# Quantised feed-forward of layer 2: its weights' and rows' FP4 rounding spread over three stages, and a new order of work in its own

## The chip, the cores and the metric

One core of a Trainium2 chip runs the whole model in one launch. The metric is the time of one execution on the device, in microseconds; before and after are compared by the median of several executions.

## The reference, cut to what matters

Four layers, each a cross attention and a feed-forward, on 2048 tokens of 256 numbers (x is 2 x 1024 x 256). Layer 0's feed-forward is a soft mixture of 8 dense experts (top 2 of the weights), layer 1's a top-2 mixture of gated experts with the rows dispatched, layer 3's a shared part and routed experts. Layer 2's is the quantised one:

```python
def fp4_quant_dequant(x):                       # blocks of 16 along the last axis
    xb = x.reshape(shape[:-1] + (shape[-1] // 16, 16))
    scale = jnp.maximum(jnp.max(jnp.abs(xb), axis=-1, keepdims=True) / 6.0, 1e-12)
    idx = jnp.searchsorted(_MID, jnp.abs(xb / scale))
    return (_GRID[idx] * jnp.sign(xb / scale) * scale).reshape(shape)

def fp4_linear(x, w):
    return jnp.einsum('bsk,nk->bsn', fp4_quant_dequant(x), fp4_quant_dequant(w))

gate = fp4_linear(x, w_gate)                    # w_gate, w_up: 704 x 256
y = fp4_linear(x, w_up)
h = jax.nn.silu(gate) * y
return fp4_linear(h, w_down)                    # w_down: 256 x 704
```

Its input x is the layer norm of the running sum. Three things are rounded to FP4: the weights, the normed rows, and the hidden rows h.

## The kernel before, in words

Tokens lie in 16 tiles of 128 (NT), four tiles to a group (NG = 4 groups). The running sum X (16 tiles x 256) and a second array Y of that size stay in SBUF, beside two arenas: FA (float32, 9216 numbers for each partition) and RA (28672). Every product in float32 is made of three matmuls of a high and a low part (split_matmuls, line 300 on; L307 is the matmul): ScalarE writes the high part, VectorE subtracts it from the value to get the low part. So each operand of TensorE passes through both engines.

The program is a list of phases, and each phase has one function for each engine; each engine's order is written out by hand, and semaphores join them. At the end of a phase all engines count on a barrier; SyncE (SP, which issues most transfers) and GpSimd wait there for all others, the compute engines go on where a phase says only_loads_wait. Each queue works in its written order, so an instruction that waits holds up all behind it on its engine.

The stages that matter here, in the order in which they run:

- Soft experts of layer 0 (gelu_block, line 1758; the jobs are lines 2045 to 2061 on VectorE and job(q, t) on TensorE). A job is one tile of tokens and two experts: six matmuls of 512 columns into one of five PSUM banks (RING = 5), then two scalar_tensor_tensors on VectorE (L2050) that add it, weighed, to X. There are four rounds (q) of 16 jobs; between the first and the second come eight bias jobs. In the last round VectorE also takes the next norm's moments (L199).
- Gated experts of layer 1 (experts, line 1410): 23 blocks (16 of 256 rows, 7 of 128). In a block TensorE makes 48 matmuls up, the transposes of the next block's rows (L1646) and 24 matmuls down for the block before. VectorE splits 1 MB of up weights (L1624) and 0.5 MB of down weights (L1693), and makes the hidden products. WeightsOfFp4 (line 501) works between its blocks: six pieces of 704 numbers, three parts each, one part after each of the blocks 1 to 18 (vector, line 542): part 0 is L548 to L553 (largest of each block of 16, scales, reciprocal, division), part 1 L555 to L557 (the exponent by a bit mask, times a magic number, added to force the rounding), part 2 L559 and L560 (subtract the magic, times the scale). GpSimd's queue loads and stores the pieces (lines 527 to 540) between the gathers and scatters of rows. The rounded pieces go to a DRAM tensor, which SP loads back (prefetch, L565) when layer 2's attention starts.
- Attention of layer 2 (attention(2), line 585): a loop of one tile a slot. VectorE's part of a slot (work, from line 870) is L876, L877 for one tile, L889, L891 for the one before, L907, L908 for the one ahead, L911, and the next norm's moments (L199, L206, L208) and minus_mean (L217). ScalarE writes the normed tiles (L225) of the norm that follows, eleven of the 16 within the loop, the last five in finish_scalar in the next stage. GpSimd has only rstd (L271), a power, once a group.
- The quantised stage (fp4_feed_forward, line 2468). First: TensorE turns the gate and up weights (L2676), ScalarE copies the high parts (L2561), VectorE makes the low parts (L2616); the down weights the same (L2682, L2563, L2564, L2618, L2620); the four groups of normed rows are quantised by VectorE (quantise_xn, line 2603, through Quantiser: L2523, L2524, L2527, L2528, L2529, L2532, then a multiplication by the magic number on ScalarE, L2556, then L2536 to L2538), turned by TensorE (L283) and split (L290, L297). Then eight pairs of tiles: gate_up for each tile (24 matmuls of 352 columns), silu on ScalarE (L2576), product on VectorE (L2629), quantising of the pair's hidden rows on VectorE (the same Quantiser on 1408 numbers), turning them (L2707), low and high parts, and the product down (L2717). The keys and the query weights of layer 3's attention (ahead[3], class Ahead) are prepared ahead of the pairs.

## Time and profile before

| | us |
|---|---|
| median of the runs | 1635.72 (1634.01 to 1636.18) |
| the profiled execution's own time | 1638.06 |
| its span, first to last instruction | 1636.3 |
| PE busy | 1386.8 (85%) |
| DVE busy | 1240.5 (76%) |
| ACT busy | 772.5 (47%) |
| POOL busy | 337.0 (21%) |

PE is TensorE, DVE VectorE, ACT ScalarE, POOL GpSimd, SP SyncE. Times in a row are microseconds from the start of the span. Line numbers are those of the kernel before. A busy share is a mean over stages with different limits. The granted clock (PEclk) of TensorE is 1.00 at 2.4 GHz and 0.50 at 1.2 GHz; values between are a stretch with both.

### The profile page before, as it was taken

How to read it: one execution, taken by the hardware profiler on the slowest of the kernel's cores; microseconds unless marked ns; L12 is line 12 of the kernel's file. 1: busy time of each engine (PE TensorE's matmuls, PEld its weight loads, DVE VectorE, ACT ScalarE, POOL GpSimd, SP SyncE). 2: the span in 40 equal slices, each digit the busy share in tenths (PEclk: the TensorE clock that was granted, in tenths of full speed). 3: DMA queues.
4: the chain of work that ended last, by engine and by line, in shares of the span. 5: the costliest groups of instructions: out<-in, count | busy, mean ns of one | idle time of the engine just before them, and what ended most of it. 6: DMA issues, size and time to landing. Idle time of an engine off the chain costs nothing.

```text
span 1636.3 us, 25886 instructions
## 1 busy us (share of the span) xinstructions
PE 1386.8 (85%) x9890; PEld 1266.5 (77%) x9890; DVE 1240.5 (76%) x2386; ACT 772.5 (47%) x1318; POOL 337.0 (21%) x278
## 2 busy tenths in 40 slices
PE   4897997798995599999399459968998999999995
PEld 4786895586883599999379358966886888999995
DVE  5696778777896589997379779976886857888773
ACT  4445442113455266666355442325445225676673
POOL 2241001000000157764100000000000013454342
PEclk9898998799998599998699879988998999999997
DMA  4232100000002478886300000000002016777784
GB/s 139 91 104 89 45 1 1 1 0 10 1 1 110 150 211 233 244 224 174 124 1 1 7 0 1 1 10 1 1 1 104 1 65 233 233 214 220 219 241 116
DMA packets 44926, 148.23 MB, mean 91 GB/s; under 512 B 11651, under 2 KB 22582, under 8 KB 35062
## 3 DMA queue, kind: packets, MB, share of 16 engines
q1 hardware_dynamic: 28886, 122.04, 21.9%
q0 software_dynamic: 15936, 24.78, 7.8%
q8 instruction: 67, 1.10, 0.3%
q14 instruction: 37, 0.30, 0.1%
HBM read 126.03 MB, written 22.87 MB: 91 GB/s over the span
## 4 chain that ended last, share of the span: by engine, by line
PE 56%; DVE 26%; ACT 8%; issue 5%; DMA 2%; POOLq 1%; SPq 1%; POOL 0%; ACTq 0%; DVEq 0%
PE PS L307 37%; PE PS L1005 6%; PE PS L966 3%; PE PS L989 3%; DVE RA L1624 2%; PE PS L1240 1%; DVE RA L1693 1%; ACT Y L225 1%; ACT RA L1617 1%; DVE FA L1661 1%; PE PS L998 1%; DVE RA L297 1%; PE PS L982 1%; DVE RA L1673 1%; POOLq L2764 1%
## 5 line engine op out<-in xcount | busy, mean ns | idle before, releaser
L307 PE MATMUL PS<-RA 128*128 128x256 f32 (+3 forms) x6204 | 942.7, 311 | 74.9 <-DVE RA L397 16.2
L307 PEld LDWEIGHTS PS<-RA 128*128 128x128 f32 x6204 | 859.5, 197 | 130.3 <-issue 34.5
L1551 POOL DMA_INDIRECT sum_rows<-Y,KT x78 | 158.6, 2033 | 193.1 <-ACT Y L1592 162.2
L271 POOL TENSOR_TENSOR rstd<-vareps,neghalf 128x4 f32<-128x4 f32 x36 | 36.8, 1023 | 707.2 <-DVE vareps L208 330.0
L1005 PE MATMUL PS<-VBF,FA 128*128 128x136 f32 x1024 | 136.1, 287 | 4.4 <-ACT FA L771 4.2
L1540 POOL DMA_INDIRECT Y<-normed_rows,KT x78 | 89.8, 1151 | 219.7 <-DVE KT L1333 158.5
L1005 PEld LDWEIGHTS PS<-VBF,FA 128*128 128x128 f32 x1024 | 124.8, 192 | 10.3 <-ACT FA L771 6.8
L771 ACT ACTIVATE FA<-PS 128x1024 f32<-128x1024 f32 x64 | 65.7, 1027 | 103.9 <-PE PS L966 103.9
L1570 ACT ACTIVATE FA<-PS,unit_bias 128x256 f32<-128x256 f32 (+1 forms) x184 | 71.7, 445 | 78.2 <-PE PS L307 65.4
L1624 DVE TENSOR_TENSOR RA<-FA,RA 128x2048 fp32r<-128x2048 f32 x46 | 105.2, 2288 | 4.4 <-ACT RA L1584 3.7
L1693 DVE TENSOR_TENSOR RA<-FA,RA 128x1024 fp32r<-128x1024 f32 (+1 forms) x46 | 80.9, 1759 | 24.8 <-ACT RA L1617 24.8
L283 PE MATMUL PS<-ident,Y 128*128 128x128 f32 x256 | 43.4, 328 | 60.2 <-ACT Y L225 33.0
L1584 ACT ACTIVATE RA<-FA 128x2048 fp32r<-128x2048 f32 x46 | 88.1, 1914 | 12.8 <-DMA FA<-in_eup 12.8
L283 PEld LDWEIGHTS PS<-ident,Y 128*128 128x128 f32 x256 | 36.8, 172 | 68.8 <-issue 45.9
L779 ACT ACTIVATE FA<-FA 128x1024 f32<-128x1024 f32 x64 | 67.5, 1055 | 39.9 <-DVE FA L908 34.6
L225 ACT ACTIVATE Y<-X,minus_mean,rstd 128x256 f32<-128x256 f32 x96 | 51.9, 590 | 63.1 <-DVE minus_mean L217 62.7
L966 PE MATMUL PS<-ident,FA 128*128 128x128 f32 x512 | 68.3, 277 | 12.0 <-ACT FA L779 12.0
L2050 DVE SCALAR_TENSOR_TENSOR X<-PS,coef,X 128x256 f32<-128x256 f32 x128 | 61.3, 482 | 19.7 <-PE PS L307 17.3
L966 PEld LDWEIGHTS PS<-ident,FA 128*128 128x128 f32 x512 | 58.5, 143 | 12.8 <-ACT FA L779 12.8
L1617 ACT ACTIVATE RA<-FA 128x1024 fp32r<-128x1024 f32 (+1 forms) x46 | 68.4, 1488 | 0.0
L989 PE MATMUL PS<-RA 64*128 64x256 f32 x768 | 63.0, 299 | 1.1 <-DVEq L902 1.1
L989 PEld LDWEIGHTS PS<-RA 64*128 64x128 f32 x768 | 50.3, 189 | 15.5 <-issue 13.8
(295 smaller groups left out, 1874.9 us busy)
## 6 DMA issues: line engine op xcount, KB each, us to landing
FA<-in_eup SPq DMA_DIRECT2D x46, 1024.0 KB, 7.0
FA<-in_edown SPq DMA_DIRECT2D x23, 1024.0 KB, 6.3
FA<-in_edown SPq DMA_DIRECT2D x23, 512.0 KB, 4.1
FA<-in_fside SPq DMA_DIRECT2D x16, 512.0 KB, 3.6
sum_rows<-X SPq DMA_DIRECT2D x2, 2048.0 KB, 7.4
normed_rows<-Y SPq DMA_DIRECT2D x2, 2048.0 KB, 10.2
fp_rows<-FA POOLq DMA_DIRECT2D x6, 352.0 KB, 6.8
FA<-fp_rows SPq DMA_DIRECT2D x1, 2112.0 KB, 11.9
```

The costliest lines, as they stand in the source:

```text
L283: ins = pe.transpose(self.bank(g, k)[:, j * P:(j + 1) * P], self.normed(g, j)[:, 0, k * P:(k + 1) * P], ident[:, :])
L307: ins = pe.matmul(dst, stat(a, k), mov(b, k), start=(first and n == 0), stop=(last and n == len(todo) - 1))
L966: ins = pe.transpose(PS[:, 4 + c // 4, (c % 4) * P:(c % 4 + 1) * P], probs[t % BUFS][:, c * P:(c + 1) * P], ident[:, :])
L989: ins = pe.matmul(PS[:, 2 * p + r, k * COLS:(k + 1) * COLS], qs[rows, a, k, t * P:(t + 1) * P], kb[rows, b, m, k, r * COLS:(r + 1) * COLS] ...
L1005: ins = pe.matmul(PS[:, 6, k * VC:(k + 1) * VC], pt[:, 4 * (c // 2) + 2 * k + c % 2, :], VB[:, t // HT, 4 * k + c, :], start=(c == 0), sto ...
L1540: pool.indirect_dma_start(out=rows_in[p][:, t, :], out_offset=None, in_=normed_rows, in_offset=bass.IndirectOffsetOnAxis(ap=source_of[:, c ...
L1551: pool.indirect_dma_start(out=sum_rows, in_=rows_out[p][:, t, :], in_offset=None, compute_op=ALU.add, out_offset=bass.IndirectOffsetOnAxis ...
L1570: ins = act.activation(h32[s % RING][:, c * BR:c * BR + w], bank[:, c * BR:c * BR + w], ACT.Relu, bias=unit_bias[:, p, 2 * s + c:2 * s + c ...
L1584: act.activation(up[q][:, 0], raw_up[q], ACT.Copy).then_inc(up_hi, 1)
L1617: act.activation(down[p][:, 0], raw_down[p], ACT.Copy).then_inc(down_hi, 1)
L1624: dve.tensor_tensor(up[q][:, 1], raw_up[q], up[q][:, 0].bitcast(F32), ALU.subtract).then_inc(up_ready, 1)
L1693: dve.tensor_tensor(down[p][:, 1], raw_down[p], down[p][:, 0].bitcast(F32), ALU.subtract).then_inc(down_ready, 1)
```

## The change

1. Weights. Pieces 0 to 3 are rounded in the soft experts, pieces 4 and 5 stay in the gated experts (blocks 1 to 6 of VectorE). SP loads and stores the early pieces; VectorE has twelve slots, one every third job from job 13 (job 13 in the first round, the others at jobs 16, 19, ..., 46, counted 16 to a round); GpSimd does the two multiplications with a value for each block, and VectorE the rest. There are two buffers for four pieces, and the slot at job 31 waits for the loads of pieces 2 and 3. The slots' order is: scales of piece 0, scales of piece 1, units of 0, rounding of 0, units of 1, rounding of 1, then the same for 2 and 3.
2. Rows. A class RowsOfFp4 splits a group's quantising: VectorE makes the scales and, in one step of two operations after the bit mask, the magic number; GpSimd does the division, the addition, the subtraction and the last multiplication. Groups 0 and 1 are done within the attention's loop (VectorE at slots 11, 12, 15 and 16; GpSimd between its rstds), groups 2 and 3 in the stage. ScalarE's magic step for rows is gone.
3. The stage's order. Only group 0 is turned before the first gate_up; the down weights are turned behind the first gate_up, in other PSUM banks; group 1 behind the second; groups 2 and 3 within the first pair; layer 3's query weights and keys in pairs 0 and 1. Buffers move in FA and Y.
4. Some semaphores are shared between stages instead of being new ones; their counts change (w_hi, w_ready, the shares).

```diff
             PIECES, PARTS, FIRST_BLOCK = 6, 3, 1
+            EARLY, FIRST_JOB, JOBS_APART = 4, 13, 3
+            def sync_early(self, sp, split):
+                sp.wait_ge(*split)
+                for n in range(2):
+                    sp.dma_start(self.early_x[n], self.source(n)).then_inc(self.early_in, 16)
+                for n in range(self.EARLY):
+                    sp.wait_ge(self.by_pool, self.multiplied(n))
+                    sp.dma_start(self.done_rows[:, n, :], self.early_x[n % 2]).then_inc(self.early_stored, 16)
+                    if n + 2 < self.EARLY:
+                        sp.wait_ge(self.early_stored, 16 * (n + 1))
+                        sp.dma_start(self.early_x[n % 2], self.source(n + 2)).then_inc(self.early_in, 16)
+            def gpsimd_early(self, pool):
+                for n in range(self.EARLY):
+                    x = self.early_x[n % 2]
+                    pool.wait_ge(self.by_vector, self.scaled(n))
+                    if n:
+                        pool.wait_ge(self.by_pool, self.multiplied(n - 1))
+                    pool.tensor_tensor(self.blocks(self.early_u), self.blocks(x), self.of_block(self.early_rs[n % 2]), ALU.mult
+                                       ).then_inc(self.by_pool, 1)
+                    pool.wait_ge(self.by_vector, self.rounded(n))
+                    pool.tensor_tensor(self.blocks(x), self.blocks(self.early_u), self.of_block(self.early_sc[n % 2]), ALU.mult
+                                       ).then_inc(self.by_pool, 1)
+            def vector_early(self, dve, steps, job):
+                slot, off = divmod(job - self.FIRST_JOB, self.JOBS_APART)
+                order = [(first + i, part) for first in range(0, self.EARLY, 2)
+                         for i, part in ((0, 0), (1, 0), (0, 1), (0, 2), (1, 1), (1, 2))]
...
+                n, part = order[slot]
+                if part == 0:
+                    dve.wait_ge(self.early_in, 32 * (n // 2 + 1))
+                    if n >= 2:
+                        dve.wait_ge(self.by_pool, self.multiplied(n - 2))
+                    self.scales(dve, steps, self.early_x[n % 2], self.early_am, self.early_sc[n % 2], self.early_rs[n % 2]
+                                ).then_inc(self.by_vector, 1)
+                elif part == 1:
+                    dve.wait_ge(self.by_pool, self.divided(n))
+                    self.units_of(dve, steps, u, m)
+                else:
+                    steps(dve.scalar_tensor_tensor(u, m, self.MAGIC, u, ALU.max, ALU.add))
+                    dve.scalar_tensor_tensor(u, m, self.MAGIC, u, ALU.max, ALU.subtract).then_inc(self.by_vector, 1)
...
+        class RowsOfFp4:
+            EARLY = 2
...
+            def vector_scales(self, dve, steps, g):
+                dve.wait_ge(fp4_norm.xn_ready, fp4_norm.groups + g + 1)
+                steps(dve.tensor_reduce(self.am, self.blocks(self.x(g)), AX, ALU.max, apply_absolute_value=True))
+                dve.tensor_scalar(self.sc[g], self.am, -1.0 / 6.0, -1e-12, ALU.mult, ALU.min)
...
+                dve.reciprocal(self.rs[g], self.rs[g]).then_inc(self.scaled, 1)
+            def vector_magic(self, dve, steps, g):
+                dve.wait_ge(self.divided, g + 1)
+                steps(dve.tensor_scalar(self.m[g].bitcast(U32), self.u.bitcast(U32), 0x7F800000, None, ALU.bitwise_and))
+                dve.tensor_scalar(self.m[g], self.m[g], self.MAGIC, self.MAGIC, ALU.mult, ALU.max).then_inc(self.magic, 1)
+            def gpsimd(self, pool, g):
+                u, m, x = self.u, self.m[g], self.x(g)
+                steps = Steps(pool, self.done, 3 * g)
+                pool.wait_ge(self.scaled, g + 1)
+                pool.tensor_tensor(self.blocks(u), self.blocks(x), self.of_block(self.rs[g]), ALU.mult).then_inc(self.divided, 1)
+                pool.wait_ge(self.magic, g + 1)
+                steps(pool.tensor_tensor(u, m, u, ALU.add))
+                steps(pool.tensor_tensor(u, m, u, ALU.subtract))
+                steps(pool.tensor_tensor(self.blocks(x), self.blocks(u), self.of_block(self.sc[g]), ALU.mult))
...
 (attention, GpSimd, l == 2)
+                        for g in range(NG):
+                            following.pool_rstd(pool, g)
+                            if 1 <= g <= rows_of_fp4.EARLY:
+                                rows_of_fp4.gpsimd(pool, g - 1)
 (attention, VectorE, at the end of a slot)
+                    if l == 2 and t in (11, 15):
+                        rows_of_fp4.vector_scales(dve, steps, (t - 11) // GT)
+                    if l == 2 and t in (12, 16):
+                        rows_of_fp4.vector_magic(dve, steps, (t - 12) // GT)
 (soft experts)
+                        weights_of_fp4.vector_early(dve, steps, NT * q + t)
 (quantised stage, ScalarE)
                 finish_scalar(act, norm, 0)
+                rows_of_fp4.wait_done(act, rows_of_fp4.EARLY - 1)
                 finish_scalar(act, norm, 1)
...
+                    if p == 0:
+                        norm.scalar(act, 2)
+                        norm.scalar(act, 3)
+                        ahead[3].scalar_query_weights(act)
+                        ahead[3].scalar_keys_hi(act)
+                    if p == 1:
+                        ahead[3].scalar_keys(act)
 (quantised stage, VectorE)
+                rows_of_fp4.vector_scales(dve, steps, 2)
+                norm.vector_lo(dve, 0)
+                rows_of_fp4.vector_scales(dve, steps, 3)
+                rows_of_fp4.vector_magic(dve, steps, 2)
...
                 product(0, 0)
+                down_weights_lo()
                 product(0, 1)
+                norm.vector_lo(dve, 1)
+                rows_of_fp4.vector_magic(dve, steps, 3)
...
+                    if p == 0:
+                        norm.vector_lo(dve, 2)
+                        norm.vector_lo(dve, 3)
+                        ahead[3].vector_query_weights(dve)
+                        ahead[3].vector_keys_lo(dve)
 (quantised stage, TensorE)
                 turn_x(0)
+                pe.wait_ge(wt_lo, 2)
+                gate_up(0, 0)
+                turn_down_weights()
+                gate_up(0, 1)
+                pe.wait_ge(wt_lo, 3)
                 turn_x(1)
-                gate_up(0, 0)
-                turn_x(2)
-                gate_up(0, 1)
-                turn_x(3)
                 gate_up(1, 0)
...
+                    if p == 0:
+                        turn_x(2)
+                        turn_x(3)
+                        pe.wait_ge(norm.xt_ready, 1 + KC * (norm.groups + NG))
```

## Rows read from the trace of the kernel before

**Rows 1.** Windows: us, busy (instructions) of each engine, PEclk, DMA share, GB/s.

```profile
373.70:394.60 20.90, 18.86 (x88) 15.47 (x87) 20.10 (x67) 6.43 (x13) 3.02 (x3) 1.00 0.00 1
...
587.50:714.20 126.70, 121.06 (x990) 118.51 (x989) 117.36 (x186) 86.94 (x170) 88.86 (x57) 1.00 0.83 232
834.00:900.00 66.00, 66.00 (x589) 60.67 (x588) 59.73 (x117) 35.51 (x47) 2.01 (x2) 0.98 0.00 1
917.00:976.00 59.00, 25.17 (x116) 23.21 (x116) 43.32 (x54) 26.88 (x50) 0.00 (x0) 0.71 0.02 5
```

**Rows 2.** Timeline of VectorE, soft experts: start, us, engine, line, instruction [idle before].

```profile
298.79 5.56 DVE L2050 SCALAR_TENSOR_TENSOR X<-PS,coef,X 128x256 f32<-128x256 f32 x12
...
341.48 1.00 DVE L2050 SCALAR_TENSOR_TENSOR X<-PS,coef,X 128x256 f32<-128x256 f32 x2 [0.35 <-PE PS L307]
```

**Rows 3.** Timeline of VectorE, one weight piece in the gated experts.

```profile
701.96 0.88 DVE L548 TENSOR_REDUCE Y<-FA 128x44 f32<-128x704 f32 x1
...
703.66 0.89 DVE L553 TENSOR_TENSOR Y<-FA,Y 128x704 f32<-128x704 f32 x1
...
713.29 0.89 DVE L557 SCALAR_TENSOR_TENSOR Y<-Y 128x704 f32<-128x704 f32 x1
```

**Rows 4.** GpSimd's groups by line: busy us, mean ns of one, idle before.

```profile
L696 POOL TENSOR_TENSOR FA<-FA,small 128x1024 f32<-128x1024 f32 x16 | 30.5, 1904 | 67.3 <-DVE small L905 67.3
```

**Rows 5.** Transfers: issues, KB each, median us from issue to landing.

```profile
FA<-in_fside SPq DMA_DIRECT2D x16, 512.0 KB, 3.6
...
fp_rows<-FA POOLq DMA_DIRECT2D x6, 352.0 KB, 6.8
```

**Rows 6.** Timeline of VectorE, gated experts: L1624 of one block and 13 blocks later.

```profile
587.51 2.29 DVE L1624 TENSOR_TENSOR RA<-FA,RA 128x2048 fp32r<-128x2048 f32 x1
...
714.21 2.29 DVE L1624 TENSOR_TENSOR RA<-FA,RA 128x2048 fp32r<-128x2048 f32 x1
```

**Rows 7.** Chain of work that ended last, layer 3's experts: start, us, what.

```profile
1387.85 11.52 PE PS L307 x96
```

**Rows 8.** Timeline of TensorE, half blocks: the transposes between up and down.

```profile
742.86 0.41 PE L1646 MATMUL PS<-ident,Y 128*128 128x128 f32 x2
...
763.16 0.41 PE L1646 MATMUL PS<-ident,Y 128*128 128x128 f32 x2
...
770.52 0.41 PE L1646 MATMUL PS<-ident,Y 128*128 128x128 f32 x2
```

**Rows 9.** Timeline of VectorE: a late slot of the attention, then group 0's quantising.

```profile
909.60 0.26 DVE L876 RECIPROCAL small<-PS 128x16 f32<-128x16 f32 x1 [1.15 <-PE PS L1005]
...
916.98 1.21 DVE L2523 TENSOR_REDUCE FA<-Y 128x64 f32<-128x1024 f32 x1
...
919.14 1.23 DVE L2529 TENSOR_TENSOR FA<-Y,FA 128x1024 f32<-128x1024 f32 x1
920.40 0.69 DVE L2532 TENSOR_SCALAR FA<-FA 128x1024 uint32<-128x1024 uint32 x1
```

**Rows 10.** Timeline of all engines, start of the quantised stage.

```profile
917.10 2.07 ACT L225 ACTIVATE Y<-X,minus_mean,rstd 128x256 f32<-128x256 f32 x4 [3.19 <-DVE minus_mean L217]
...
922.09 2.56 ACT L2561 ACTIVATE RA<-PS 128x1408 fp32r<-128x1408 f32 x2
...
925.88 3.15 DVE L2616 TENSOR_TENSOR RA<-PS,RA 128x1408 fp32r<-128x1408 f32 x2
929.08 2.82 PE L2682 MATMUL PS<-ident,FA 128*128 128x128 f32 x12 [12.64 <-DVE RA L2616]
...
946.79 5.05 PE L307 MATMUL PS<-RA 128*128 128x352 f32 x24
...
976.29 4.07 PE L307 MATMUL PS<-RA 128*128 128x352 f32 x24 [1.86 <-DVE FA L2629]
```

**Rows 11.** Timeline of VectorE: where the first and the second pair's quantising start.

```profile
976.06 1.61 DVE L2523 TENSOR_REDUCE FA<-FA 128x88 f32<-128x1408 f32 x1
...
989.62 1.61 DVE L2523 TENSOR_REDUCE FA<-FA 128x88 f32<-128x1408 f32 x1
```

More of the change, by code:

```diff
@@ L520, in source, with blocks, of_block, scales @@
                 return A["fp4_down"][:, n - (self.PIECES - KC), :]
+            def blocks(self, v):
+                return v.rearrange("p (b i) -> p b i", i=FB)
+            def of_block(self, v):
+                return v.unsqueeze(2).to_broadcast([P, FI // FB, FB])
+            def scales(self, dve, steps, x, am, sc, rs):
+                steps(dve.tensor_reduce(am, self.blocks(x), AX, ALU.max, apply_absolute_value=True))
+                dve.tensor_scalar(sc, am, -1.0 / 6.0, -1e-12, ALU.mult, ALU.min)
+                more = 1.0 + 2.0 ** -22
+                steps(dve.tensor_scalar(rs, am, more / 6.0, more * 1e-12, ALU.mult, ALU.max))
+                return dve.reciprocal(rs, rs)
@@ L2239, in shared_feed_forward @@
             before = 2
+            halves_before = before + KC
             norm = relu_norm
@@ L2446, in tensor @@
                 go_down(0, 3)
-                pe.wait_ge(w_ready, before + 2)
+                pe.wait_ge(w_ready, halves_before + 2)
                 go_up(1, 0)
@@ L2484, in fp4_feed_forward @@
             h = fview(2048, 3, PT * FI)
-            act_g = fview(6336, 2, FI)
-            scale, rscale, amax = (fview(7808 + n * P, P) for n in range(3))
+            act_g = fview(7296, 2, FI)
+            scale, rscale, amax = (fview(n * P, P) for n in range(3))
             yf = Y[:, :, :].rearrange("p t d -> p (t d)")
-            units, magic = (yf[:, o:o + 2048] for o in (0, 2048))
+            units = yf[:, 0:PT * FI]
+            magic_of = lambda p: yf[:, 2048:2048 + PT * FI] if p else h[:, 2, :]
             MAGIC = 1.5 * 2.0 ** 22
-            x_units, x_magic = fview(0, GT * D), fview(GT * D, GT * D)
             q_done = sem(n_ + "done")
@@ L2548, in fp4_feed_forward, with gpsimd @@
             tile_of = lambda p, i: PT * p + i
+            def gpsimd(pool):
+                for g in range(rows_of_fp4.EARLY, NG):
+                    rows_of_fp4.gpsimd(pool, g)
             def scalar(act):
                 finish_scalar(act, norm, 0)
+                rows_of_fp4.wait_done(act, rows_of_fp4.EARLY - 1)
                 finish_scalar(act, norm, 1)
@@ L2653, in vector @@
                     dve.wait_ge(h_done, PT * (p + 1))
-                    q = Quantiser(steps, h[:, p % 3, :], units, magic)
+                    q = Quantiser(steps, h[:, p % 3, :], units, magic_of(p))
                     q.normalise()
@@ L2678, in tensor, with turn_down_weights @@
                     ins.then_inc(wt_ready, 1)
[L2679 to L2684 removed]
+                def turn_down_weights():
+                    pe.wait_ge(norm.xt_ready, 1 + KC * (norm.groups + 1))
+                    for c in range(CK):
+                        for k in range(KC):
+                            ins = pe.transpose(turned_d[0:CW[c], c * D + k * P:c * D + (k + 1) * P], raw_down[:, k, c * P:c * P + CW[c]], ident[:, :])
+                    ins.then_inc(wt_ready, 1)
                 def turn_x(g):
[L2687 removed]
+                    rows_of_fp4.wait_done(pe, g)
                     norm.tensor(pe, g)
```

169 lines of the change are left out of this document (87 added, 82 removed).

## The prediction

> **What bounds the kernel now.** First the windows by stage. In the gated experts' loop VectorE is busy 117.36 of 126.70 us, TensorE 121.06, at full clock: the DMA share is 0.83, so both engines are near their limit there [rows 1]. In the soft experts (lines 2045 to 2073) the bound changes: for the first three quarters VectorE waits for TensorE before every job (0.35 us), and in the last quarter, where the next norm's moments are taken too, it is busy 20.10 of 20.90 [rows 1, 2]. In layer 2's attention loop it is busy 59.73 of 66.00; in the 59 us ahead of the quantised stage's pairs it is busy 43.32 and TensorE only 25.17, at 0.71 of the full clock [rows 1]. That last stretch is a chain through four engines, not a busy engine. Then the timelines of those four places, for where VectorE waits and for whom. The profiled execution took 1638.06 us (span 1636.3), 2.3 over the median of 1635.72; I work out a difference and apply it to the median. A measurement of this kernel tells about 0.2% (3.3 us) from no change.
>
> **Part 1: four of six weight pieces move into the soft experts.** A piece costs VectorE there: the scales 1.70 us (start of L548 to start of L553 [rows 3]), the units about 1.1 (two tensor_scalars, at 704/1024 of the price in part 3 and a gap each), two scalar_tensor_tensors of 0.89 with 0.04 between, so 1.85 [rows 3]. Two multiplications go to GpSimd, at 704/1024 of 1.90, 1.31 us each [rows 4]. That is 4.6 us of VectorE for each piece, 18.4 for four, in twelve slots, one every third job. What is there to cover it: a TensorE-bound job takes 1.36 us, back to back VectorE needs 5.56/12 x 2 = 0.93, so 0.43 is free [rows 2]. The slot at job 13 has two jobs behind it before the bias rows, on which TensorE waits: 1.7 - 0.9 = 0.8 is exposed. The other eleven slots hold 16.7 us, the 32 jobs of the second and third quarter free 13.8: 2.9 are left, and nothing in the last quarter takes them back [rows 1].
> A new wait: the slot at job 31 needs pieces 2 and 3, and piece 3 is loaded only after piece 1 is stored, which GpSimd finishes after the slot at job 28. On SP's queue: 1.31 multiply, a 352 KB store, a wait for it, a 352 KB load. The nearest idle-queue transfer took 3.6 us for 512 KB; under the experts' traffic 352 KB took 6.8 [rows 5]. The queue is idle here, so I take 3.6 and 3.4, 8.5 us with semaphores, from one store alone to 6.8 twice (15). Three jobs at 0.93 pass meanwhile: VectorE waits 8.5 - 2.8 = 5.7 us. Behind this wait stand all later jobs; TensorE's five buffers don't help, because VectorE itself has no time left to catch up. Sum 0.8 + 2.9 + 5.7 = **+9 us** (ends +5 and +16). SP has nothing else queued until the stage ends, and GpSimd's next item, the next norm's rstd, comes after the last slot.
> A sentence on a page: by the Trainium skill, page "DMA: Bandwidth & Descriptors", section "Anatomy of one DMA", a transfer costs about 2.0 us plus its bytes over 436 GB/s, 2.8 for 352 KB, which would make this part 7.5; that fit is for GpSimd's queue.
>
> **Part 2: the gated experts keep two pieces, in blocks 1 to 6.** Whole blocks now take (714.21 - 587.51)/13 = 9.75 us [rows 6]. TensorE alone needs 72 matmuls of 0.12 and four transposes, some 0.5: 9.1 [rows 7, 8]. Blocks 7 to 15 become TensorE's: at most 0.65 each; at least what TensorE is idle now, 5.64/13 = 0.43 [rows 1]. I take 0.6, nine times, 5.4. In the half blocks the transposes of three blocks lie 20.30 us apart for two periods and 7.36 for the third; that third is a half block with no piece at full clock, and the 20.30 hold a piece and a fall of the clock [rows 8]. With no piece and the clock held, a half block takes 7.4: 5.5 us off the two in the 20.30, and some 2 off the two before them. If the fall stays, 4 in all. I take 6. Sum **-11.5** (-8 to -14). GpSimd issues four stores and four loads less; its queue ends nothing here, so that is 0.
>
> **Part 3: two groups of rows within the attention loop.** VectorE's scales take 919.14 - 916.98 = 2.16, the magic step two tensor_scalars of 0.69, 1.4 [rows 9]. At slots 11 and 12 the loop has no gap, so 2.0 + 1.4. At slot 15 there is 1.15 us of idle ahead of L876 [rows 9]: 1.0 is left. At slot 16 the gap is shorter; 0.7. Sum **+5** (+3 to +8).
>
> **Part 4: the quantised stage.** Two groups' quantising leaves VectorE altogether, the two others' but for scales and magic step (3.6 each). But the stretch is a chain, so I follow it, from VectorE's end of the attention (0). GpSimd's last three operations on group 1 at 1.9 start 2 us before: they end at 4.3. Its rstd of group 3 is queued behind them: 5.5 (it was 1.1). ScalarE's four tiles wait for both: 7.7. The two weight copies, 2.56: 10.4. VectorE's low halves, the second 1.6 later: 12.3 [rows 4, 10]. Scales of group 2, 2.2: 14.5. The low half of group 0: 15.8. gate_up 5.0, as the first one took after such a start: 20.8 [rows 10]. Weights of down turned, 2.8: 23.6 [rows 10]. gate_up 5.4 (my estimate, between 4.1 at full clock and 8.1 at half, near the row of 5.05): 29.0. Silu and product, 1.7, and gate_up 5.4: 36.2; silu and product: the first pair starts at 38. Before, it started at 976.06, with the attention's end 1.2 us ahead of 916.98, so after 60.3 [rows 9, 11]: -22.3.
> Back in: pair 0. Groups 2 and 3 are turned behind gate_up(2, 0), whose result needs 44 + 4.1 = 48; silu, ScalarE's copy, four low halves and the layer 3 weights on VectorE end at 54, then it rounds (5): the next pair starts at 60, 22 us after the first, which was 13.6 [rows 11]: +8.3. ScalarE's work on layer 3's keys now sits between pairs 1 and 2 and delays a silu; VectorE waited for nothing there: I take +1.3. The six later pairs don't change. Stage: **-12.7** (-16 to -4).
>
> **Sum**: 9 - 11.5 + 5 - 12.7 = -10.2 us.
>
> **Rivals.** (a) GpSimd and VectorE in each other's way: layer 0 runs GpSimd's 1.90 us operation beside VectorE, every one alike, but not beside a VectorE operation with two operands in SBUF [rows 4]. If such operations exclude each other, each that meets GpSimd waits up to 1.9 us: L891 in two slots, the magic steps, the first pair's normalise, some 2 to 6, say +4: -6, 1629.5. For it: the change puts twelve GpSimd operations of 1024 beside VectorE. Against it: most stand where VectorE waits anyway.
> By the Trainium skill, page "SBUF — State Buffer", section "SBUF: two separate sides", the two engines share a pair of ports as an exclusive lock, which VectorE takes with two SBUF inputs or in its 2-port mode: that is this rival, and no row here shows it either way.
> (b) Experts don't give it back: ScalarE or the queues end the blocks (DMA share 0.83 of the stretch already [rows 1]), 9 x 0.2 and the clock's fall stays: -5 in place of -11.5. With part 1 at 11 us: -2, 1634.
> (c) Slower: TensorE stays at its lower clock. It is idle 13 us ahead of the first gate_up (12.64 before a stretch at 0.71 now [rows 1, 10]). A gate_up at the lower clock is 8.1 against my 5.0 to 5.4 for three, and 4.1 for the four of the first two pairs: 9 + 16 = 25 on the chain, less 1 or 2 that VectorE's own work covers. The net is then +13, 1649. It decides from about 13 us, that is if most of these seven are slow. Against it: the first gate_up after such a start took 5.05, the one of the first pair 4.07 [rows 10].
> (d) That it doesn't do what it says: the diff does move the work, the slots are compiled in and each has its semaphore, so I give this nothing of its own; a time within 0.2% would come by (b), where the parts cancel.
>
> **Chances.** Forecast 0.48, (a) 0.22, (b) 0.17, (c) 0.13. The forecast is the median less 10: 1625.7 us. Its own range is 1616 to 1632; (a) and (b) reach 1636; cutting off (c) and 5 parts in 100 at the low end gives 1614 to 1638. Faster by over 0.2% (below 1632.4): most of the forecast and of (a), 0.3 of (b): 0.70. Within 0.2%: 0.17. Slower: (c), 0.13.
>
> **What would show it.** Right: VectorE's L2050 jobs stand back to back from job 16, one wait of 4 to 7 us on a DMA at job 31, the stage ends 9 us later; whole blocks from the seventh at 9.1 to 9.2 and no fall of the clock in the half blocks; the attention 5 us longer; GpSimd busy some 4 us into the stage, the first pair 38 us after the attention and the second 22 after that. Wrong: blocks still at 9.7; GpSimd operations over 1.9 or VectorE's two-operand ones stretched, which is (a); gate_ups at 8 us, which is (c).

## The result, and the profile after

The kernel before took 1635.92 us (median of 12 runs), the changed one 1630.85 (12 runs): ratio 0.9969, 95% interval 0.996 to 0.9978, so 5.1 us or 0.31% faster. In a later comparison on one chip it was 0.9963 (0.995 to 0.9977). The forecast said 10.2 us faster; the measured time lies inside its range, but the gain is half of what the sum gave. The profiled execution took 1628.77 us (span 1627.0), the shortest of its kernel's runs and 2.1 under their median, while the one of before was 2.1 over its own; the two profiles differ by 9.3 us, and 4 of that is which runs were profiled. Two single executions at a low clock, 6883.65 us in e2 and 2324.21 us in e4, are left out of the ratios and medians below.

Windows of the kernel after: the last quarter of the soft experts, whole blocks of the gated experts, the end of layer 2's attention, and from there to the quantised stage's first pair. They answer to [rows 1].

```profile
377.50:398.40 20.90, 16.09 (x72) 13.18 (x71) 20.13 (x68) 6.43 (x13) 3.02 (x3) 0.98 0.04 17
590.00:716.70 126.70, 124.55 (x1033) 123.36 (x1033) 108.87 (x167) 93.27 (x176) 86.14 (x55) 1.00 0.80 224
858.00:921.00 63.00, 53.42 (x424) 48.30 (x422) 58.57 (x113) 28.74 (x41) 17.54 (x9) 0.92 0.00 1
921.00:954.50 33.50, 18.21 (x100) 17.23 (x100) 16.55 (x26) 11.53 (x16) 16.74 (x9) 0.80 0.02 8
```

The bound changed as foreseen in two places: in the gated experts TensorE is now busy 124.55 of 126.70 us and VectorE 108.87 (117.36 before), and the stretch ahead of the first pair is 33.5 us where it was 60.3. The attention is the surprise. VectorE is busy 58.57 of its last 63 us and TensorE only 53.42, where the window of before had TensorE busy throughout and VectorE 59.73 of 66.

Soft experts, timelines of SP and of VectorE: the store of piece 1 and the load of piece 3 behind it, and the wait at job 31.

```profile
347.14 0.33 SPq L556 DMA_DIRECT2D fp_rows<-FA  x1
349.38 0.33 SPq L559 DMA_DIRECT2D FA<-in_fp_gate_up  x1
```

```profile
345.56 2.82 DVE L2182 SCALAR_TENSOR_TENSOR X<-PS,coef,X 128x256 f32<-128x256 f32 x6
352.33 0.89 DVE L540 TENSOR_REDUCE FA<-FA 128x44 f32<-128x704 f32 x1 [3.95 <-DMA FA<-in_fp_gate_up]
```

One wait on a DMA, where the prediction put it; the store took 2.2 us and the load 3.0, against 3.6 and 3.4 assumed.

Gated experts, timeline of VectorE (once a whole block) and of TensorE (the transposes of the half blocks), as in [rows 6, 8]:

```profile
669.40 2.29 DVE L1754 TENSOR_TENSOR RA<-FA,RA 128x2048 fp32r<-128x2048 f32 x1 [0.58 <-ACT RA L1714]
...
678.47 2.29 DVE L1754 TENSOR_TENSOR RA<-FA,RA 128x2048 fp32r<-128x2048 f32 x1 [0.58 <-ACT RA L1714]
```

```profile
743.26 0.40 PE L1776 MATMUL PS<-ident,Y 128*128 128x128 f32 x2
...
750.62 0.40 PE L1776 MATMUL PS<-ident,Y 128*128 128x128 f32 x2
```

Whole blocks come every 9.07 us (9.75 before), half blocks every 7.36, at full clock.

Then the attention, timeline of VectorE: every operation of two lines that took longer than in the kernel before, where the first of them (L1017 here, L891 there) took 0.48 and L208 0.17.

```profile
887.32 1.35 DVE L1017 SCALAR_TENSOR_TENSOR X<-FA,gates,X 128x256 f32<-128x256 f32 x1
...
894.04 1.78 DVE L1017 SCALAR_TENSOR_TENSOR X<-FA,gates,X 128x256 f32<-128x256 f32 x1
...
899.32 0.79 DVE L208 TENSOR_SCALAR vareps<-meanvar 128x4 f32<-128x4 f32 x1
...
911.32 1.35 DVE L1017 SCALAR_TENSOR_TENSOR X<-FA,gates,X 128x256 f32<-128x256 f32 x1
...
916.52 2.21 DVE L1017 SCALAR_TENSOR_TENSOR X<-FA,gates,X 128x256 f32<-128x256 f32 x1
...
919.64 1.38 DVE L208 TENSOR_SCALAR vareps<-meanvar 128x4 f32<-128x4 f32 x1
```

And the timeline of GpSimd there:

```profile
886.46 1.93 POOL L689 TENSOR_TENSOR VD<-Y,KT 128x1024 f32<-128x1024 f32 x1 [10.30 <-DVE KT L678]
893.13 2.41 POOL L691 TENSOR_TENSOR VD<-Y,VD 128x1024 f32<-128x1024 f32 x1 [4.74 <-DVE Y L683]
895.61 2.46 POOL L692 TENSOR_TENSOR VD<-Y,VD 128x1024 f32<-128x1024 f32 x1
898.15 1.94 POOL L693 TENSOR_TENSOR Y<-VD,KT 128x1024 f32<-128x1024 f32 x1
900.25 1.02 POOL L271 TENSOR_TENSOR rstd<-vareps,neghalf 128x4 f32<-128x4 f32 x1 [0.17 <-DVE vareps L208]
910.46 1.93 POOL L689 TENSOR_TENSOR VD<-Y,KT 128x1024 f32<-128x1024 f32 x1 [9.19 <-DVE KT L678]
916.06 2.39 POOL L691 TENSOR_TENSOR VD<-Y,VD 128x1024 f32<-128x1024 f32 x1 [3.67 <-DVE Y L683]
918.53 2.46 POOL L692 TENSOR_TENSOR VD<-Y,VD 128x1024 f32<-128x1024 f32 x1
921.07 1.93 POOL L693 TENSOR_TENSOR Y<-VD,KT 128x1024 f32<-128x1024 f32 x1
923.08 1.02 POOL L271 TENSOR_TENSOR rstd<-vareps,neghalf 128x4 f32<-128x4 f32 x1
```

Read the ends against each other. GpSimd's operation at 886.46 ends at 888.39 and VectorE's at 887.32 at 888.67; 895.54 and 895.82; 912.39 and 912.67; 918.45 and 918.73: each time VectorE ends 0.28 us behind GpSimd. L208 at 899.32 ends at 900.11, with GpSimd's of 898.15 (900.09), and at 919.64 it ends at 921.02, with GpSimd's of 918.53 (920.99). That is rival (a), in the plainest form: in these rows VectorE's operation is not over before GpSimd's is. The six rows hold 6.6 us more than they would at 0.48 and 0.17. Not every operation is held: beside the same GpSimd operations those with an operand in PSUM (L1015, 0.41; L1033, 1.21) and the moments, which read one operand from SBUF (L199, 0.41), keep their length, and so does L1017 at 901.09 (0.48) beside the rstd of 900.25.

The quantised stage, timelines of VectorE and of TensorE, as in [rows 10, 11]:

```profile
924.13 0.16 DVE L217 SCALAR_TENSOR_TENSOR minus_mean<-meanvar,rstd 128x4 f32<-128x4 f32 x1 [3.12 <-POOL rstd L271]
...
954.50 1.61 DVE L2657 TENSOR_REDUCE FA<-FA 128x88 f32<-128x1408 f32 x1
...
956.26 1.96 DVE L2661 TENSOR_SCALAR FA<-FA 128x88 f32<-128x88 f32 x1
...
976.99 1.61 DVE L2657 TENSOR_REDUCE FA<-FA 128x88 f32<-128x1408 f32 x1
```

```profile
934.20 6.80 PE L307 MATMUL PS<-RA 128*128 128x352 f32 x24 [12.04 <-DVE RA L297]
...
942.86 4.07 PE L307 MATMUL PS<-RA 128*128 128x352 f32 x24 [0.55 <-DVE FA L2758]
...
976.30 2.79 PE L2841 MATMUL PS<-ident,FA 128*128 128x128 f32 x12 [7.99 <-DVE FA L2672]
978.74 5.17 PE L307 MATMUL PS<-RA 128*128 128x352 f32 x24
```

After 12.04 us of idle the first gate_up takes 6.80 us at a granted clock of 0.56 of full speed, and the others up to the first pair 4.07; so rival (c) did not come. The price of the new order is TensorE's 7.99 us of idle in pair 0, while VectorE does what was moved there. VectorE is held up once more here: L2661, on 88 numbers a row, takes 1.96 us at 956.26 and 0.20 a pair later (978.76), and ends at 958.22 with a GpSimd multiplication that ran from 956.22 to 958.16. It takes 1.95 to 1.97 in all eleven kernels with the new stage.

### The profile page after: what moved, and what is told of

It is laid out like the page before. It is cut to its first block, busy times and chain, and to the rows that moved or that the text cites. A ratio compares the mean times of both kernels' runs of the same rounds, so it can differ in the third digit from the quotient of the medians.

```text
span 1627.0 us, 25891 instructions
## 1 busy us (share of the span) xinstructions
PE 1381.6 (85%) x9890; PEld 1263.5 (78%) x9890; DVE 1222.4 (75%) x2366; ACT 768.9 (47%) x1314; POOL 369.0 (23%) x294
## 4 chain that ended last, share of the span: by engine, by line
PE 59%; DVE 24%; ACT 7%; issue 4%; DMA 3%; POOL 1%; POOLq 1%; SPq 1%; ACTq 0%; DVEq 0%
PE PS L307 40%; PE PS L1135 6%; PE PS L1096 3%; PE PS L1119 3%; DVE X L2182 2%; PE PS L1370 1%; DVE RA L297 1%; ACT Y L225 1%; PE PS L1128 1%; POOLq L2904 1%; PE PS L1112 1%; PE PS L1776 1%; DVE RA L1754 1%; ACT RA L482 1%; DMA FA<-in_Wo 1%
## 5 line engine op out<-in xcount | busy, mean ns | idle before, releaser
L1681 POOL DMA_INDIRECT sum_rows<-Y,KT x78 | 151.4, 1941 | 196.9 <-ACT Y L1722 166.4
L1754 DVE TENSOR_TENSOR RA<-FA,RA 128x2048 fp32r<-128x2048 f32 x46 | 105.3, 2288 | 10.9 <-ACT RA L1714 10.7
```

The source lines that it names most:

```text
L1681: pool.indirect_dma_start(out=sum_rows, in_=rows_out[p][:, t, :], in_offset=None, compute_op=ALU.add, out_offset=bass.IndirectOffsetOnAxis ...
L1754: dve.tensor_tensor(up[q][:, 1], raw_up[q], up[q][:, 0].bitcast(F32), ALU.subtract).then_inc(up_ready, 1)
```

## The experiments

The table gives the profiled execution of each by stretches (us): **soft** from job 12 of the soft experts to SP's issue of layer 1's Wo; **gated** from the router's loads to the loads of X; **attention** from there to VectorE's last moments in layer 2's attention; **first pair** and **next** from there to the first and on to the second pair's quantising; **stage** the whole from the attention's end to SP's issue of layer 3's Wo. The last column is the ratio of times to the kernel before; e1 to e4, e5 to e8 and e9 to e12 ran on one chip each, with the kernel before beside them.

| kernel | soft | gated | attention | first pair | next | stage | ratio |
|---|---|---|---|---|---|---|---|
| before | 81.3 | 287.2 | 122.7 | 60.3 | 13.6 | 184.9 | 1 |
| after | 87.3 | 276.4 | 132.4 | 33.5 | 22.5 | 170.9 | 0.9969 |
| e4, after again | 88.4 | 276.3 | 132.6 | 33.4 | 24.0 | 172.6 | 0.9963 |
| e1 weights only | 89.0 | 276.4 | 121.7 | 60.4 | 13.7 | 187.5 | 0.9989 |
| e2 rows only | 80.7 | 287.4 | 133.3 | 33.4 | 24.0 | 172.5 | 0.9989 |
| e3 four buffers | 84.9 | 275.0 | 132.3 | 33.3 | 24.1 | 172.4 | 0.9943 |
| e5 no GpSimd rows | 88.7 | 276.3 | 125.6 | 30.9 | 24.1 | 170.3 | 0.9933 |
| e6 no VectorE rows | 87.3 | 278.3 | 128.4 | 31.5 | 22.5 | 169.1 | 0.9936 |
| e7 one group | 88.9 | 276.3 | 127.7 | 31.7 | 24.0 | 170.8 | 0.9930 |
| e8 e3 and e7 | 84.2 | 274.9 | 129.5 | 30.6 | 24.1 | 169.6 | 0.9893 |
| e9 bias in PSUM | 88.3 | 276.4 | 126.7 | 36.0 | 24.0 | 175.1 | 0.9934 |
| e10 e8 and e9 | 83.3 | 275.7 | 124.0 | 31.9 | 22.5 | 169.5 | 0.9867 |
| e11 e10, all layers | 84.3 | 274.7 | 125.0 | 31.1 | 24.0 | 170.5 | 0.9873 |
| e12 idle operations | 81.4 | 288.8 | 123.7 | 60.2 | 12.5 | 183.9 | 1.0014 |

Between kernels that share its code, the attention repeats to 1.0 us, soft and next to 1.7, gated to 2.0 and the old stage to 3.6 (183.9 to 187.5). The time from the start to job 12, the same code in all, varies from 312.4 to 315.9, and what follows the stage, nearly the same in all, from 532.2 to 539.9. The longest of these is e7's, whose profiled execution is 6.8 us over its median.

**e1**, the diff's hunks on the weight pieces alone:

> The kernel before with parts 1 and 2 of the change alone (four weight pieces in the soft experts, two in the gated experts; rows and quantised stage as before). Theory A, read from the two profiles: the soft experts cost 6.1 us, the gated experts give back 10.8, and the fall of the clock in the first attention (2.6) is chance: 4.7 us less than the kernel before, ratio 0.997. Theory B: that fall comes with the moved pieces, so it is in this kernel's profile too and the gain is 2 us, 0.999. My forecast's own terms said +9 - 11.5, 2.5 us less.

1634.32 us, ratio 0.9989 (0.998 to 0.9998), 1.8 less (1.0 by the medians). In number that is B, but not in kind: layer 1's attention takes 110.7 us here, 109.9 before and 112.5 in the changed kernel's profile, so B's fall of the clock is not there. **e2**, the hunks on the rows and the stage alone:

> The kernel before with parts 3 and 4 alone (two groups' rows in the attention loop, the quantised stage in its new order; all six weight pieces in the gated experts). Theory A, read from the profiles: attention 2 costs 9.7 us to VectorE's end, the stage gives 13.9: 4.2 us less. Theory B, my forecast's terms: +5 - 12.7, 7.7 less. Under A the operations of VectorE with two operands in SBUF (0.49 us before) take 1.3 to 2.2 us beside GpSimd's four operations for each group, as in the profile after; under B the stretches there came from the weight pieces' change and are gone.

1634.2 us, 0.9989 (0.998 to 0.9998). The two stretches of each half are those of the changed kernel (89.0 and 276.4; 133.3 and 172.5), and the operations stretched in e2's attention as well: in these stretches the halves don't act on each other, and part 3's price has nothing to do with the weights. B's 7.7 for e2 is out. In time each half gave less than A read from the profiles, by 2.9 and 2.4 us. For e1 its profile shows where it went: the quantised stage, whose code e1 leaves alone, takes 187.5 us and not 184.9. Its end alone, from the last pair's quantising on, takes 27.1 us at a granted clock of 0.75, before 25.0 at 0.87. All twelve executions of e1 have a mean granted clock of 0.911 to 0.918, where the kernel before beside them has 0.919 on average. Why it is lower there is not shown, so e1's 1.8 us is not a clean price of the weights' move.

**e3**, early_x with four buffers:

```
-self.early_x = [fview(at, FI) for at in (0, FI)]
+self.early_x = [fview(at, FI) for at in (0, FI, 6912, 7616)]
...
+sp.wait_ge(self.by_vector, self.scaled(1))
+for n in range(2, self.EARLY):
+    sp.dma_start(self.early_x[n], self.source(n)).then_inc(self.early_in, 16)
...
-    if n + 2 < self.EARLY:
-        sp.wait_ge(self.early_stored, 16 * (n + 1))
-        sp.dma_start(self.early_x[n % 2], self.source(n + 2)).then_inc(self.early_in, 16)
```

> The changed kernel, but pieces 2 and 3 go into buffers of their own, loaded once the scales of piece 1 are taken, so that the slot at job 31 waits for no store and load. Theory A: the one wait of 3.95 us there ends, nothing else makes TensorE or VectorE late, and the soft experts end 4 us sooner: 4 us less than the changed kernel. Theory B: VectorE's wait was partly covered (TensorE is up to five jobs ahead) and the time goes into waits for TensorE: 0 to 1.5 us less. If the first attention's clock falls again (0.59 for 6 us), it does not depend on when the stage ends.

> The changed kernel again, as the measure for the others on this chip, and for a second profile of it. Theory A (parts add up): about the sum of the two half changes, -4.7 and -4.2, so 9 us less than the kernel before, and the 5.1 us of the first comparison were low by chance. Theory B: 5 us less again, and one of the two halves gives less than its profile says; if the low clock of the first attention is in this profile too, that is a cost of the change.

Ratio 0.9943 (0.9924 to 0.9962), e4 0.9963 on the same chip; medians 1626.24 and 1630.44, 4.2 apart. The wait is gone and the soft stretch is 3.5 us shorter: A. e4 gave about the first comparison's gain again (6.1 by the ratio, 4.9 by the medians), not 9: its B, and both halves gave less than their profiles said. Layer 1's attention takes 110.6 us in e4, so the 112.5 is not what the change costs each time.

**e5** and **e6** take the two engines' work on groups 0 and 1 apart. In gpsimd() and in vector_scales() and vector_magic() the operations give way to bare increments of their semaphores:

> The changed kernel, but GpSimd leaves out its four operations on each of groups 0 and 1 (those rows stay unquantised); VectorE's scales and magic steps stay in their slots. Theory A, the two engines exclude each other where VectorE reads two operands from SBUF or runs a fast form: in attention 2 every subtraction of the split is back at 0.49 us, VectorE's part of the attention costs 4 to 5 us instead of 9.7, and the stage starts 3 us sooner because the next norm's rstd waits for nothing: 7 to 9 us less than the changed kernel, ratio 0.991 to 0.992. Theory B, the stretches are something else (the longer program, the moved weights) and the attention's cost is the added VectorE work: the subtractions still stretch, and only the 3 us of the rstd go, 0.9945.

> The changed kernel, but VectorE leaves out its scales and magic steps for groups 0 and 1 (those rows come out wrong); GpSimd does all its operations. Theory A: VectorE's own subtractions and moments still meet GpSimd's operations and stretch by up to 2 us each, so of the 9.7 us of the attention some 5 stay, though no VectorE work is added; the time falls by 4 to 5 us. Theory B: without the added VectorE work nothing is left of the 9.7, and the time falls by 8 to 10.

VectorE's groups by line in the last 44 us of the attention (line, operation, names, shapes, count; busy us, mean ns; idle before). The kernel after:

```profile
L1017 DVE SCALAR_TENSOR_TENSOR X<-FA,gates,X 128x256 f32<-128x256 f32 x7 | 8.1, 1164 | 0.2
L1034 DVE TENSOR_TENSOR FA<-PS,small 128x1024 f32<-128x1024 f32 x5 | 6.1, 1224 | 0.2
...
L208 DVE TENSOR_SCALAR vareps<-meanvar 128x4 f32<-128x4 f32 x2 | 2.2, 1084 | 0.1
```

e5, without GpSimd's operations:

```profile
L1039 DVE TENSOR_TENSOR FA<-PS,small 128x1024 f32<-128x1024 f32 x5 | 6.1, 1224 | 0.2
...
L1022 DVE SCALAR_TENSOR_TENSOR X<-FA,gates,X 128x256 f32<-128x256 f32 x7 | 3.4, 484 | 0.2
...
L208 DVE TENSOR_SCALAR vareps<-meanvar 128x4 f32<-128x4 f32 x2 | 0.3, 170 | 0.1
```

e6, without VectorE's:

```profile
L1023 DVE SCALAR_TENSOR_TENSOR X<-FA,gates,X 128x256 f32<-128x256 f32 x7 | 7.6, 1085 | 0.2
...
L208 DVE TENSOR_SCALAR vareps<-meanvar 128x4 f32<-128x4 f32 x2 | 1.1, 538 | 0.1
```

The operation that adds the tile to X goes from 1164 ns to 484 without GpSimd and stays at 1085 without VectorE's added work. The one with an operand in PSUM (L1034, 1224 ns) is never touched. VectorE's end of the attention (before 122.7) is 125.6 with its own work alone, 128.4 with GpSimd's alone, 132.4 with both: +2.9, +5.7 and +9.7. Theory A on both counts, though VectorE's own work costs less than A's 4 to 5 us. In time e5's ratio of 0.9933 (0.9918 to 0.9948) lies between A and B and settles nothing: it is 4.9 us under e4's, where its stretches gave 9.3 (attention 7.0, stage 2.3, where VectorE waits less for the rstd). In its profile 2.9 of the rest went behind the stage (536.6 us, e4 533.7), in code that is the same. e6 is at 0.9936 (0.9918 to 0.9954), 4.4 us under e4's ratio, as A had it; its attention ends 4.2 sooner.

**e7**, one group wholly in the loop (EARLY = 1 for the rows; GpSimd's division of group 1 behind the rstd of group 2, VectorE's magic step of group 1 first in the stage, GpSimd's other three operations there). **e8** adds e3's edit.

> The changed kernel, but only group 0 is quantised wholly in the attention loop; of group 1 the scales and the division stay there, and its magic step and GpSimd's other three operations come in the stage, behind the rstd of group 3. Theory A: two of eight meetings in the loop with a two-operand VectorE operation go (1.5 to 3 us), the magic step leaves the loop (0.7), and ScalarE's last tiles no longer wait 3 us for the rstd; the groups 2 and 3 come 4 us later, which the wait between the first and second pair mostly has room for: 3 to 5 us less than the changed kernel, ratio 0.994. Theory B: the chain of the stage takes the delay on (groups 2 and 3 late by 4 us at the turn behind the fifth gate_up): no gain.

> Both edits to the changed kernel: the four buffers (3.4 us less in the soft experts' stretch of the earlier run) and the one group. They lie in separate stages, so they should add: Theory A 7 to 9 us less than the changed kernel, ratio 0.9915 to 0.9925. Theory B, one group gives nothing: 0.9945. In the first attention the clock held for the whole stage with four buffers and fell with two; if that is the rule the clock holds here.

e7: 1623.32 us, 0.9930 (0.9917 to 0.9944), 5.4 us less than e4 by the ratios; the attention ends 4.9 us sooner and the first pair 1.7 after that. e8: 1617.39 us, 0.9893 (0.9878 to 0.9909). They add, and by more than expected (11.5 us under e4 by the ratios, 7 to 9 expected).

**e9** keeps all work and moves one operand:

```
-steps(dve.tensor_tensor(tmp, y, bo_row, ALU.add))
+with_bias = y if l == 2 else tmp
+steps(dve.tensor_tensor(with_bias, y, bo_row, ALU.add))
 x = X[:, bass.ds(t, 1), :]
-dve.scalar_tensor_tensor(x, tmp.unsqueeze(1), gates[:, l:l + 1], x, ALU.mult, ALU.add).then_inc(fin_done, 1)
+dve.scalar_tensor_tensor(x, with_bias.unsqueeze(1), gates[:, l:l + 1], x, ALU.mult, ALU.add).then_inc(fin_done, 1)
```

> The changed kernel, but in layer 2's attention VectorE leaves the tile with its bias in PSUM, in place, instead of in SBUF, so that the operation that adds it to X has one operand in SBUF and not two. GpSimd's and VectorE's work is the same in number. Theory A (it is two operands in SBUF that meet GpSimd): the seven of the last 44 us of the attention, 1165 ns each on average in the changed kernel, come back under 500, VectorE's part of the attention is 4 to 5 us shorter (132.5 after the loads of X, now 128), and the time falls by 4 to 5 us, ratio 0.9935. The moments' last operation (1.1 us instead of 0.17) still meets GpSimd. Theory B (any VectorE operation on SBUF is held up): nothing changes, or the wait moves to the next operation.

VectorE's groups by line, the same part of e9's attention:

```profile
L1018 DVE SCALAR_TENSOR_TENSOR X<-PS,gates,X 128x256 f32<-128x256 f32 x7 | 3.4, 484 | 0.2
L1016 DVE TENSOR_TENSOR PS<-PS,FA 128x256 f32<-128x256 f32 x7 | 3.0, 426 | 0.1
...
L208 DVE TENSOR_SCALAR vareps<-meanvar 128x4 f32<-128x4 f32 x2 | 0.9, 458 | 0.1
```

484 ns each, beside the same GpSimd operations (five of the seven run wholly within one, as that at 914.77 within GpSimd's of 914.47 to 916.88): it is the second operand in SBUF. The attention ends at 126.7, 5.9 us sooner, and the ratio is 0.9934 (0.9914 to 0.9954), as A had it. What it did not foresee: 2.6 us are given back ahead of the first pair (36.0), where ScalarE's tiles wait for GpSimd's rstd of group 3. That sits behind group 1's operations, and their end moves less than VectorE's.

> The kernel with four buffers and one group in the loop, and layer 2's biased tile in PSUM. Theory A: VectorE's part of the attention from 129 to 126 or 127, 2 to 3 us less than that kernel (1617.4, ratio 0.9893), so ratio 0.9875. Theory B: none, 0.9893. The clock of the first attention holds, as in the two kernels with four buffers so far (109.9 us for the stage).

> As the last, with the biased tile in PSUM in all of layers 1 to 3. In layers 1 and 3 no GpSimd work runs beside it, so by Theory A only the operation's own time counts there: the same, or 0.07 us less a tile if reading PSUM is as quick as in the operations at 0.42: 0 to 2 us in all. Theory B: a gain in layers 1 and 3 as large as in layer 2 would mean that the form, and not GpSimd, made the difference.

e10: 1614.13 us, 0.9867 (0.9844 to 0.989), the fastest of all: by the ratio 21.8 us under the kernel before. e11: 0.9873 (0.9849 to 0.9896), no gain in layers 1 and 3, where no GpSimd work runs beside: in layer 3 the operation takes 0.48 us in either form. The first attention took 110.2 and 110.1 us in the two, 109.9 in e3 and e8, at a mean granted clock of 0.93 to 0.94 in all four.

**e12**, operations of GpSimd that nobody waits for, added to the kernel before:

```
+spare = VD[:, 1].rearrange("p b d -> p (b d)")
+idle = Steps(pool, sem(n_ + "idle%d" % l))
+for g in range(NG):
+    following.pool_rstd(pool, g)
+    for _ in range(8 if g in (1, 2) else 0):
+        if l == 2:
+            idle(pool.tensor_tensor(spare, spare, spare, ALU.add))
+        elif g == 1:
+            idle(pool.tensor_scalar(spare, spare, 1.0, None, ALU.mult))
+        else:
+            idle(pool.memset(spare, 0.0))
```

> The kernel before with GpSimd operations that nothing waits for and no other change: in layer 2's attention eight additions of 512 elements a row behind the rstd of group 1 and eight behind that of group 2; in layer 3's eight scalings with one operand behind that of group 1 and eight fills with none behind that of group 2. Theory A: in layer 2 VectorE's operations with two operands in SBUF that meet an addition take up to its length (some 1.2 us) more, 0.48 to about 1.0 on average, and layer 2's attention is 2 to 4 us longer; the scalings do the same in layer 3, the fills, which read nothing, leave that operation at 0.48. Theory B (GpSimd's operations cost VectorE nothing by themselves): both attentions keep their 123 and 128 us. With the next norm's rstd behind the operations, up to 1 us each may also come from that.

Timelines of e12: GpSimd's runs of additions, scalings and fills, and VectorE's L903 (X) and L217 within them. L217 is a scalar_tensor_tensor too, with both operands in SBUF, four numbers a row.

```profile
884.49 9.19 POOL L709 TENSOR_TENSOR VD<-VD 128x512 f32<-128x512 f32 x8
...
904.94 9.11 POOL L709 TENSOR_TENSOR VD<-VD 128x512 f32<-128x512 f32 x8
...
1192.96 12.51 POOL L711 TENSOR_SCALAR VD<-VD 128x512 f32<-128x512 f32 x8
...
1215.67 4.60 POOL L713 MEMSET VD<- 128x512 f32 x8
```

```profile
887.54 0.51 DVE L217 SCALAR_TENSOR_TENSOR minus_mean<-meanvar,rstd 128x4 f32<-128x4 f32 x1
...
889.37 1.18 DVE L903 SCALAR_TENSOR_TENSOR X<-FA,gates,X 128x256 f32<-128x256 f32 x1
...
894.81 0.49 DVE L903 SCALAR_TENSOR_TENSOR X<-FA,gates,X 128x256 f32<-128x256 f32 x1
...
909.74 1.18 DVE L903 SCALAR_TENSOR_TENSOR X<-FA,gates,X 128x256 f32<-128x256 f32 x1
...
1192.93 0.93 DVE L903 SCALAR_TENSOR_TENSOR X<-FA,gates,X 128x256 f32<-128x256 f32 x1
...
1196.49 0.26 DVE L217 SCALAR_TENSOR_TENSOR minus_mean<-meanvar,rstd 128x4 f32<-128x4 f32 x1
...
1198.59 0.48 DVE L903 SCALAR_TENSOR_TENSOR X<-FA,gates,X 128x256 f32<-128x256 f32 x1
...
1204.25 0.63 DVE L903 SCALAR_TENSOR_TENSOR X<-FA,gates,X 128x256 f32<-128x256 f32 x1
...
1218.69 0.15 DVE L217 SCALAR_TENSOR_TENSOR minus_mean<-meanvar,rstd 128x4 f32<-128x4 f32 x1
```

The two L903 that begin inside a run of additions take 1.18 us, the one after it 0.49: A in kind. L217 takes 0.51 there, twice (the second at 907.91), and 0.15 alone; it ends with the addition (888.05, the addition 888.03). In size A was too high. Only these four operations in 18 us of additions waited for one, 2.1 us together, and the attention ends 1.0 later than before, not 2 to 4, which is no more than it differs between before and e1; the time rose by 2.3 us (1.0014, 1.0 to 1.0029), part of it outside this stretch.

In these rows scalings hold VectorE for less than their length. They follow each other every 1.57 us and take 1.49, so the starts are 1192.96, 1196.12 (the third), 1197.70 (the fourth) and 1203.99 (the eighth). The L903 of 1192.93 ends 0.90 us after the first started, that of 1204.25 0.89 after the eighth; that of 1198.59, which begins 0.89 after the fourth started, takes its usual 0.48; L217 of 1196.49 ends 0.63 after the third started. With the 0.28 by which L1017 ended behind an operation that held it, a scaling held VectorE for about its first 0.6 us, by my estimate from these four rows. Layer 3's attention kept its 128.2 us. One operation met a fill: L217 of 1218.69 runs wholly within one and takes its usual 0.15. So one that reads nothing did not hold VectorE up there; it is a single case.

## Why the prediction was right or wrong

**What bounds the kernel**: right for the soft experts, the gated experts and the quantised stage. For the attention the prediction named VectorE (59.73 of 66.00 us) and left out that TensorE was busy for all of the 66.00 [rows 1].

**Part 1**, +9 forecast. The soft stretch is 87.3 to 89.0 us in the seven kernels with two buffers, 88.3 on average, and 81.1 in the three without early pieces: +7.2. With four buffers it is 84.2, so +3.0 for the slots (0.8 + 2.9 forecast) and 4.1 for the wait (5.7 forecast), which in after's profile is the 3.95. The step held; the transfers were quicker. (The prediction's terms add to 9.4, which it wrote as 9.) By the page "DMA: Bandwidth & Descriptors" of the Trainium skill, section "Anatomy of one DMA", this part was to be 7.5 (with 2.8 for each of the two transfers its terms give 8.0); the load's 2.95 us from issue to VectorE's start agrees with the page's 2.8, on SP's queue as well, while the store's 2.24 from its issue to that of the load behind it is under it.

**Part 2**, -11.5 forecast: -10.9, by the steps foreseen (9.07 a block, half blocks at 7.4).

**Part 3**, "Sum +5 (+3 to +8)": this step failed. It priced the added VectorE work and took everything else in the loop to keep its length. The added work, 7.1 us of VectorE, is worth +2.9 (e5), not 5. The other 5.7 to 7 come with GpSimd's eight operations, six of which hold up a VectorE operation that reads two operands from SBUF (L1017) or is the tensor_scalar L208; 6.6 us of it stand in the six rows above. Together that is +9.7. This was rival (a), given 0.22, a price of 4 us and a time of 1629.5, with the argument against it that most such operations stand where VectorE waits anyway. In the loop VectorE is idle for only 4.4 of the last 63 us. And the rival's list had L891 in two slots, the magic steps and the first pair's normalise; it was L891 in four slots, L208 in two, and in the first pair L2661, while the magic steps and the normalise kept their length. The sentence of the Trainium skill, page "SBUF — State Buffer", section "SBUF: two separate sides", that the two engines share a pair of ports as an exclusive lock, is borne out: by the ends 0.28 us apart, by e5, and by e9, where one operand leaves SBUF and the wait goes. That it is held for the whole instruction, as the page has it, agrees with the additions and multiplications here, but not with the scalings of e12 (about 0.6 of 1.49 us), nor with L1017 at 901.09, which began 0.84 us into an rstd of 1.02 and was not held.

**Part 4**, -12.7 forecast. From VectorE's end of the attention the stage gives -13.9 in after's profile and -12.3 to -12.5 in three others with the same code, all against before's 184.9, which itself was 183.9 and 187.5 in the two others with the old code. That the total fits is in part luck, since within it the errors cancel. The first pair is at 33.5, not 38: VectorE's end had itself moved 5 us later, while GpSimd's operations on group 1 ran on, so they ended 2.0 us behind it and not 4.3, and the gate_ups took 6.80 and then 4.07 each, where I had 5.0 and then 5.4. The next pair starts 22.5 to 24.1 later (22 forecast), and the three pairs after that cost 4 to 5 us more than before (1.3 forecast). In after's profile 2.5 of that is in the first of them, where TensorE comes out of 7.99 us of idle at a lower clock, 0.77 granted: the turning takes 2.79 us and the gate_up 5.17 instead of 1.53 and 4.07, and VectorE waits 2.46 for the silu behind them. This is read from the profile and no run tests it.

**The sum** by stretches is 7.2 - 10.9 + 9.7 - 12.5 = -6.5 us, the forecast's -10.2 with part 3 twice as dear and the rest within 2 us. The two comparisons measured -5.1 and -6.1. Each half alone gave 1.8 where its stretches say 3.7 and 2.8. For e1 the rest goes with the lower clock in code that it leaves alone, whose cause is open; for the others the rest of about 1 us is not explained, and the stretches outside the change vary by more than that. The execution of after that was profiled also had the clock at 0.59 for 6 us in layer 1's attention (112.5 us for the stage, 109.9 before); over the other kernels that stage takes 109.8 to 111.8, with the second largest in e12, which has no early pieces. I take it for chance and not for a cost of the change; no run settles it.

## What to carry to other kernels

Work given to GpSimd beside a busy VectorE is not free for VectorE: count the VectorE operations with two operands in SBUF that will run in that time, and the small tensor_scalars with their one, and price each meeting at up to the length of GpSimd's instruction (less for the one-operand scalings of e12, nothing for its one fill). If one operand of such an operation can stay in PSUM, the meeting costs nothing (e9, 5.9 us of VectorE's time for one changed line). When an engine has little idle time, a wait put into it, such as a store and reload through one buffer, is paid nearly in full (e3: 3.5 of 3.95 us).

## What the runs showed of the hardware

GpSimd's addition of 1024 elements a row with two full operands takes 2.36 to 2.46 us, a multiplication with one of them broadcast 1.93; on 512 elements an addition takes 1.04, a scaling with one operand 1.49, a fill 0.52, with 0.06 to 0.08 to the next. A VectorE tensor_scalar on four elements a row, 0.17 us alone, took up to 1.38 beside GpSimd, and one on 88 took 1.96 instead of 0.20: small operations pay as much as large ones. It is not the small size alone: the moments' last sums (L206, two numbers a row, 0.15) kept their length beside the same GpSimd operations. With four buffers the gated stretch, whose code is the same, is 0.6 to 1.7 us shorter in all four kernels (274.7 to 275.7, against 276.3 to 276.4 in six kernels with two buffers and 278.3 in e6); I found no reason.
